# Expert stage: the first product of one tile issued in turn with the second product of the tile two behind it

## The reference, cut to what matters

```
logits = xn @ Wr + br;  top_p, top_idx = top_k(softmax(logits), 2);  weights = top_p / sum(top_p)
h = gelu(einsum('end,edh->enh', xn * ln_g + ln_b, W1) + b1)     # D=256 -> H=1024
y = einsum('enh,ehd->end', h, W2) + b2                          # H=1024 -> D=256
out = sum over the two chosen experts of weights * y;  x = x + out
```

## Time and profile before

| | us |
|---|---|
| median of 3 runs | 1185.47 (1185.44 to 1186.91) |
| the profiled execution | 1184.77 |
| its span in the trace | 1182.8 |
| expert stage, first `turn` to the last matmul | 821 to 1169 |
| TensorE busy over the span | 897.8 (76%) |
| VectorE, ScalarE, GpSimd busy | 740.9, 667.1, 671.8 |

### The profile page before, as it was taken

How to read it: one execution, slowest core, us unless ns; L and a number is a source line. 1 busy time by engine, 2 the same in 40 slices (tenths; PEclk the granted TensorE clock), 3 DMA queues, 4 the chain that set the end, 5 groups by cost and what they waited for, 6 DMA issues and landing times.

```text
span 1182.8 us, 25502 instructions
## 1 busy us (share of the span) xinstructions
PE 897.8 (76%) x6921; PEld 600.9 (51%) x6922; DVE 740.9 (63%) x1644; ACT 667.1 (56%) x2181; POOL 671.8 (57%) x678
## 2 busy tenths in 40 slices
PE   3284877687767866676776869525999999999995
PEld 1031433353324323354555648525777777777773
DVE  4667786878668755685556588865445555555543
ACT  7986996398935996352332336415444444444442
POOL 3753777767777777777773621326244444444442
PEclk9986997888878998686656889757999999999998
DMA  4113333443333333445442435411122222222221
GB/s 132 57 61 111 105 99 94 95 130 94 100 103 103 98 103 100 141 130 171 135 133 66 135 94 160 135 44 58 24 42 43 44 44 44 44 40 43 43 45 23
DMA packets 59608, 102.47 MB, mean 87 GB/s; under 512 B 10298, under 2 KB 43048, under 8 KB 59400
## 3 DMA queue, kind: packets, MB, share of 16 engines
q0 software_dynamic: 29520, 65.96, 23.0%
q1 hardware_dynamic: 30008, 35.55, 9.3%
HBM read 84.27 MB, written 17.20 MB: 86 GB/s over the span
## 4 chain that ended last, share of the span: by engine, by line
PE 46%; ACT 17%; DVE 16%; DMA 8%; issue 6%; POOL 4%; DVEq 2%; SPq 1%; POOLq 0%; ACTq 0%
ACT Wall L1045 10%; PE bank L979 9%; DMA Wall<-xl_d,gbuf 6%; PE bank L967 6%; PE bank L969 5%; PE bank L968 4%; ACT RB L1053 4%; PE bank L981 4%; POOL Wall L661 3%; PE bank L822 3%; PE bank L835 2%; PE bank L787 2%; PE bank L824 2%; PE bank L823 2%; DVE RA L1520 2%
## 5 line engine op out<-in xcount | busy, mean ns | idle before, releaser
L661 POOL DMA_INDIRECT Wall<-xl_d,gbuf x391 | 398.7, 1020 | 153.3 <-issue 75.9
L1053 ACT ACTIVATE RB<-RB,gbuf 128x128 f16<-128x128 f16 x488 | 178.4, 424 | 196.0 <-DVE RB L1507 196.0
L1045 ACT ACTIVATE Wall<-Wall 128x128 f32<-128x128 f16 (+1 forms) x782 | 246.5, 382 | 8.0 <-DVE Wall L1438 7.8
L822 PE MATMUL bank<-Wall,RB 128*128 x488 | 156.9, 322 | 113.6 <-DMA Wall<-xl_d,gbuf 44.6
L715 POOL DMA_INDIRECT out_dram<-RA,slot_tok x56 | 88.8, 1586 | 188.6 <-ACT RA L1171 181.6
L1520 DVE TENSOR_TENSOR RA<-RA,bank 128x256 f32 x244 | 101.9, 418 | 146.5 <-PE bank L824 135.4
L787 PE MATMUL bank<-Wall 128*128 128x512 f16 (+1 forms) x391 | 147.3, 421 | 30.3 <-ACT Wall L1045 24.3
L969 PE MATMUL bank<-RA,Wall 128*128 128x128 f16 x896 | 168.9, 223 | 0.0
L967 PE MATMUL bank<-RA,Wall 128*128 128x128 f16 x896 | 168.4, 223 | 0.5 <-issue 0.3
L968 PE MATMUL bank<-RA,Wall 128*128 128x128 f16 x896 | 166.6, 221 | 0.0
L822 PEld LDWEIGHTS bank<-Wall,RB 128*128 128x128 f16 x488 | 54.5, 112 | 213.4 <-issue 200.9
(11 more groups left out here) (314 smaller groups left out, 1570.6 us busy)
## 6 DMA issues: line engine op xcount, KB each, us to landing
stage<-in_L_ffn_W SPq DMA_DIRECT2D x10, 1024.0 KB, 5.2
Wall<-xl_d,gbuf POOLq DMA_INDIRECT x391, 2.8
Wall<-in_L_ffn_W SPq DMA_DIRECT2D x6, 1024.0 KB, 6.2
Wall<-in_x SPq DMA_DIRECT2D x4, 640.0 KB, 6.8
xl_d<-Wall SPq DMA_DIRECT2D x4, 640.0 KB
out_dram<-RB SPq DMA_DIRECT2D x4, 640.0 KB
xn_d<-RA SPq DMA_DIRECT2D x4, 640.0 KB
RB<-in_x SPq DMA_DIRECT2D x1, 1792.0 KB
```

Source lines behind the costliest of these rows:

```text
L661: pool.indirect_dma_start(out=ring[:, t % RING * 2 * D:(t % RING + 1) * 2 * D], out_offset=None, in_=xl_d, in_offset=bass.IndirectOffsetOn ...
L822: mm(o, high, ring[:, bass.ds(at, D)], start=True, stop=False)
L1045: last = act.activation(hi_word[:, n % SR, k * S:(k + 1) * S], hi_hot[:, n // HB % 2, n % HB // 2, 0:S, n % 2], ACT.Copy, scale=pay[k][:, ...
L1053: act.activation(low, high, ACT.Copy, scale=rec_r[:, n:n + 1]).then_inc(sw_built, 1)
```

## The change

The second product of tile t is issued in turn with the first product of tile t+2: an eighth of `up` (6 matmuls), an eighth of `down` (2 matmuls), eight times. For that `up` runs two tiles ahead instead of one, `turn` three instead of two, GpSimd's gather is moved one ahead (its fifth before the loop), and the orders of ScalarE and VectorE follow: `x_high(t+3)`, `gelu(t+2)`, `y_scale(t)`; `h_parts(t+1)`, `x_low(t+3)`, `y_rows(t)`. The word of a group holds 6 digits instead of 5. The number of matmuls and of tile buffers is the same. Before the loop now stand `up(0)` and `up(1)`; after it only `down` of the last two tiles stands alone.

```
@@ gpsimd
             for t in range(XR):
                 gather(t)
+            pool.wait_ge(ft_mm, 2 + 1)
+            gather(XR)
             for t in range(FT):
-                if t + XR < FT:
-                    pool.wait_ge(ft_mm, 2 + t + 1)
-                    gather(t + XR)
+                if t + XR + 1 < FT:
+                    pool.wait_ge(ft_mm, 2 + t + 2)
+                    gather(t + XR + 1)
@@ tensor
+            def up_part(t, q, e, hc):
+                if hc == 0:
+                    pe.wait_ge(fx_split, 2 + t + 1)
+                if hc % 4 == 0:
+                    pe.wait_ge(gelu_done, 2 * t + hc // 4 + 1)
+                o = bank[2 * q + hc // 4][:, (hc % 4) * P:(hc % 4) * P + P]
+                for kc in range(KC):
+                    w = [Wall[:, bass.ds(e + (part * KC + kc) * H + hc * P, P)] for part in range(2)]
+                    xh, xo = xhi[q][:, kc * P:kc * P + P], xlo[q][:, kc * P:kc * P + P]
+                    mm(o, w[0], xh, start=kc == 0, stop=False)
+                    mm(o, w[0], xo, start=False, stop=False)
+                    m = mm(o, w[1], xh, start=False, stop=kc == KC - 1)
+                if hc % 4 == 3:
+                    m.then_inc(up_mm, 1)
+
+            def down_part(t, q, ew2, hc):
+                if hc == 0:
+                    pe.wait_ge(y_out, t + 1)
+                    pe.wait_ge(h_split, 2 + t + 1)
+                w = Wall[:, bass.ds(ew2 + hc * 2 * D, 2 * D)]
+                hh, hl = hhi[q][:, hc * P:hc * P + P], hlo[q][:, hc * P:hc * P + P]
+                if hc == HC - 1:
+                    mm(bank[4 + q][:, 0:D], hl, Wall[:, bass.ds(ew2 + hc * 2 * D, D)], start=False, stop=False)
+                m = mm(bank[4 + q][:, 0:2 * D], hh, w, start=hc == 0, stop=hc == HC - 1)
+                if hc < HC - 1:
+                    mm(bank[4 + q][:, 0:D], hl, Wall[:, bass.ds(ew2 + hc * 2 * D, D)], start=False, stop=False)
+                else:
+                    m.then_inc(down_mm, 1)
...
+            def up_and_down(tu, qu, exu, td, qd, exd):
+
+                e = pe.snap(exu * WE)
+                ew2 = pe.snap(exd * WE + W2BASE)
+                for hc in range(HC):
+                    up_part(tu, qu, e, hc)
+                    down_part(td, qd, ew2, hc)
...
-            up(0, 0, experts(0)[0])
+            ex = experts(0)
+            up(0, 0, ex[0])
+            turn(2, 2, 1)
+            up(1, 1, ex[1])
             pe.wait_ge(w_done, 4 * NE)
             with pe.Fori(0, FT // XR - 1) as i:
                 ex = experts(i)
                 for q in range(XR):
-                    turn(XR * i + q + 2, (q + 2) % XR, i + 1 + (q + 2) // XR)
-                    up(XR * i + q + 1, (q + 1) % 2, ex[q + 1])
-                    down(XR * i + q, q % 2, ex[q])
+                    turn(XR * i + q + 3, (q + 3) % XR, i + 1 + (q + 3) // XR)
+                    up_and_down(XR * i + q + 2, q % 2, ex[q + 2], XR * i + q, q % 2, ex[q])
...
@@ scalar
                 for q in range(XR):
-                    x_high(XR * i + q + 2, q % 2)
-                    gelu(XR * i + q + 1, (q + 1) % 2, word, q + 1)
+                    x_high(XR * i + q + 3, (q + 1) % 2)
+                    gelu(XR * i + q + 2, q % 2, word, q + 2)
                     y_scale(XR * i + q, q % 2)
@@ vector
-            digit = [... for k in range(XR + 1)]
+            digit = [... for k in range(XR + 2)]
...
                 for q in range(XR):
-                    x_low(XR * i + q + 2, q % 2)
                     h_parts(XR * i + q + 1, (q + 1) % 2)
+                    x_low(XR * i + q + 3, (q + 1) % 2)
                     y_rows(XR * i + q, q % 2, word, q)
```

More of the change, by code:

```diff
@@ L952, in experts @@
             def experts(group):
-                word = pe.value_load(exp_tab[0:1, bass.ds(group, 1)], min_val=0, max_val=NE ** (XR + 1) - 1)
-                return [(word // NE ** k) % NE for k in range(XR + 1)]
+                word = pe.value_load(exp_tab[0:1, bass.ds(group, 1)], min_val=0, max_val=NE ** (XR + 2) - 1)
+                return [(word // NE ** k) % NE for k in range(XR + 2)]
+            def up_part(t, q, e, hc):
[12 more added lines that the diff above has]
+                    m.then_inc(up_mm, 1)
@@ L957, in up @@
             def up(t, q, ex):
                 e = pe.snap(ex * WE)
[L959 to L970, removed]
+                for hc in range(HC):
+                    up_part(t, q, e, hc)
@@ L972, in down @@
             def down(t, q, ex):
                 ew2 = pe.snap(ex * WE + W2BASE)
-                pe.wait_ge(y_out, t + 1)
-                pe.wait_ge(h_split, 2 + t + 1)
                 for hc in range(HC):
[L977 to L984, removed]
@@ L985, in down @@
-                m.then_inc(down_mm, 1)
+                    down_part(t, q, ew2, hc)
+            def up_and_down(tu, qu, exu, td, qd, exd):
+                e = pe.snap(exu * WE)
+                ew2 = pe.snap(exd * WE + W2BASE)
+                for hc in range(HC):
+                    up_part(tu, qu, e, hc)
+                    down_part(td, qd, ew2, hc)
+            assert HC == 8
             turn(0, 0, 1)
             turn(1, 1, 1)
-            up(0, 0, experts(0)[0])
+            ex = experts(0)
@@ L999, in _ @@
                 t = FT - XR + q
+                if t + 3 < FT:
+                    turn(t + 3, (t + 3) % XR, (t + 3) // XR + 1)
                 if t + 2 < FT:
[L1001 to L1004, removed]
+                    up_and_down(t + 2, t % 2, ex[q + 2], t, t % 2, ex[q])
+                else:
+                    down(t, t % 2, ex[q])
         @block.scalar
@@ L1156, in expert_word @@
             def expert_word(group):
-                return act.value_load(exp_tab[0:1, bass.ds(group, 1)], min_val=0, max_val=NE ** (XR + 1) - 1)
+                return act.value_load(exp_tab[0:1, bass.ds(group, 1)], min_val=0, max_val=NE ** (XR + 2) - 1)
             def gelu(t, q, word, k):
@@ L1174, in _ @@
             x_high(1, 1)
-            gelu(0, 0, expert_word(0), 0)
+            word = expert_word(0)
+            gelu(0, 0, word, 0)
+            x_high(2, 0)
+            gelu(1, 1, word, 1)
             with act.Fori(0, FT // XR - 1) as i:
@@ L1178, in _ @@
                 for q in range(XR):
-                    x_high(XR * i + q + 2, q % 2)
-                    gelu(XR * i + q + 1, (q + 1) % 2, word, q + 1)
+                    x_high(XR * i + q + 3, (q + 1) % 2)
+                    gelu(XR * i + q + 2, q % 2, word, q + 2)
                     y_scale(XR * i + q, q % 2)
             word = expert_word(FT // XR - 1)
[L1183 to L1188, removed]
+            for q in range(XR):
+                t = FT - XR + q
+                if t + 3 < FT:
+                    x_high(t + 3, (t + 3) % 2)
+                if t + 2 < FT:
+                    gelu(t + 2, t % 2, word, q + 2)
+                y_scale(t, t % 2)
         @block.vector
@@ L1713, in _ @@
             link(dve.memset(exp_row[:, FT:FT + XR], 0.0))
-            digit = [exp_row[:, k:k + FT].rearrange("p (g k) -> p g k", k=XR)[:, :, 0] for k in range(XR + 1)]
+            digit = [exp_row[:, k:k + FT].rearrange("p (g k) -> p g k", k=XR)[:, :, 0] for k in range(XR + 2)]
             words = exp_row[:, FT + XR:]
-            for k in range(XR, 0, -1):
-                link(dve.scalar_tensor_tensor(out=exp_tab[:, :] if k == 1 else words, in0=digit[XR] if k == XR else words,
+            for k in range(XR + 1, 0, -1):
+                link(dve.scalar_tensor_tensor(out=exp_tab[:, :] if k == 1 else words, in0=digit[XR + 1] if k == XR + 1 else words,
                                               scalar=float(NE), in1=digit[k - 1], op0=ALU.mult, op1=ALU.add))
@@ L1759, in expert_word @@
             def expert_word(group):
-                return dve.value_load(exp_tab[0:1, bass.ds(group, 1)], min_val=0, max_val=NE ** (XR + 1) - 1)
+                return dve.value_load(exp_tab[0:1, bass.ds(group, 1)], min_val=0, max_val=NE ** (XR + 2) - 1)
             def y_rows(t, q, word, k):
@@ L1774, in _ @@
             h_parts(0, 0)
+            x_low(2, 0)
             dve.wait_ge(b2_in, 16)
@@ L1784, in _ @@
                 t = FT - XR + q
-                if t + 2 < FT:
-                    x_low(t + 2, t % 2)
                 if t + 1 < FT:
                     h_parts(t + 1, (t + 1) % 2)
+                if t + 3 < FT:
+                    x_low(t + 3, (t + 3) % 2)
                 y_rows(t, t % 2, word, q)
```

## The result

| | before | after |
|---|---|---|
| median of 20 runs, us | 1184.22 | 1188.91 |
| ratio | | 1.004, 95% interval 1.0022 to 1.0059 |
| span of the profiled execution | 1182.8 | 1188.6 |
| a pass of the loop, mean of 12 | 24.26 | 24.41 |

The change made the kernel 4.7 us slower, by 2.6 to 7.0; 4.4 were forecast.

What follows compares the result with a forecast made beforehand. The prediction took TensorE's sequencer, not its array, to bound the expert stage; 2.5 + 0.1 + 0 + 1.8 = +4.4 us gave 1189.2 on the profiled execution, 1189.9 for the median, range 1183 to 1195.

Steps and rivals of the forecast that it cites:

- The bound: Expert stage: TensorE's sequencer sets the pass at 24.3 us, whatever the instructions' order; the array needs 21.96.
- (c): Waits between TensorE, ScalarE and VectorE in the loop: existing cover, 2.5 us ahead of `down`, suffices; 0 us.
- The first rival: Array itself pauses after each third first-product matmul, so long matmuls hide loads: some -31 us, 1154 us; chance 0.12.
- (a): `down` of a pass's first tile: two wait values computed afresh for one bare wait gone, 0.09 us a pass.
- (b): `down` of a pass's second tile: expert decoded again, six register operations instead of three, +0.10 us a pass.
- (d): Kernel's end: tile 53's scaling and output DMA come later, delaying the chain that ends last, +1.8 us.
- The pauses: TensorE's loop: pauses become smaller and more frequent, the period stays; tiles not first in a pass take 5.7 to 5.8 us.
- The last rival: TensorE alternating short and long matmuls: each change of kind costs array time, 1250 us, or 1199 at 0.03 us; chance 0.07.

Runs made afterwards that it cites:

- kernel 1: Changed kernel, both weight addresses of each three first-product matmuls computed in one register instruction, against the changed kernel: 22.29 us a pass, 1159.71 us, 0.9793 of before.
- kernel 8: Changed kernel plus one more address instruction in each eighth of the first product, same matmuls: 28.64 us a pass, 1.0456 of before.
- kernel 7: Changed kernel with fixed weight addresses on TensorE, the choice of expert left out in both products: 21.99 us a pass, 0.9787 of before.
- kernel 2: Kernel before, with both weight addresses of each three first-product matmuls computed in one register instruction: 23.81 us a pass, 1173.97 us, 0.9912 of before.
- kernel 4: Changed kernel, but at its end tile 53's second product and scaling go ahead of tile 55's first product and gelu: 1187.12 us, 1.0037 of before.
- kernels 3: Changed kernel with its new tile order, but eighths not in turn, all of up(t+2) then all of down(t): 1188.16 us, 1.0035 of before.
- kernel 5: Changed kernel with shared address instructions and new tile order, but eighths not in turn: 21.99 us a pass, 0.9787 of before.
- kernel 11: Changed kernel, eighths in turn, with shared address instructions and the old order at the end: 22.30 us a pass, 0.9799 of before.

## Why the prediction was right

- **The bound.** That the sequencer and not the array sets the changed kernel's pass was shown: 61 instructions fewer gave 2.1 us a pass (kernel 1), 32 more cost 4.23 (kernel 8), and none leaves the array's 21.99 (kernel 7). In the kernel before the same 61 are worth only 0.45 us a pass (kernel 2), for the reason under (c). The first rival, that the pause is the array's own, is out, and with it the pace of about 81 ns a matmul of the Trainium skill, page "TensorE: Matmul & The Clock Gate", section "Back-to-back issue gap", for this stream: 42 loads and matmuls ran at 0.0555 us before, and kernel 7's whole pass fits that pace.
- **(a) and (b).** Forecast +0.19 us a pass; measured 24.41 - 24.26 = 0.15, 13 passes +2.0 us for 2.5. The sequencer's rows show the added instructions at the places named.
- **(c).** The forecast of 0 held, but for a weaker reason than I gave, so partly by luck. I read a cover of 2.5 us ahead of `down` and took it for slack. But the chain through ScalarE and VectorE turns in 5.75 us, and the three tiles of a pass that have no branch took (24.26 - 7.00) / 3 = 5.75: there the two bounds are level. Only in the first tile did ScalarE wait for TensorE (both waits 12 times, once a pass, where it waited for VectorE 46 times, once a tile):

```profile
ACT RA L1171 <- DVE RA L1770: 134.2, 46, 3.0
ACT RA L1154 <- PE bank L969: 8.5, 12, 0.8
ACT RA L1165 <- PE bank L969: 2.5, 12, 0.3
```

  These are its waits between 860 and 1140 us: in total, times, longest. I read the cover as what that tile gives back in each pass; no run varied it. Over a pass the bounds are 24.26 and 23.81, one behind the other. The change took the second apart, which could not show while the first stood.
- **(d).** Forecast +1.8, measured +2.1 from the last matmul to the last DMA. The mechanism, a late scaling and then DMAs from landing to issue, is in the rows and starts where I put it: tile 53's DMA 3.1 us ahead of the last matmul's start, forecast (1166.3 and 1169.44) and measured (1170.00 and 1173.08). Each step from issue to issue was then put at 4.58 us; they measured 4.75 and 4.57. What I didn't see is how close ahead of it tile 52's DMA stands, so that kernel 4's repair of tile 53 alone gained nothing.
- **The pauses.** I wrote that they become smaller and more frequent, and that the tiles other than the first of a pass take 5.7 to 5.8 us. Both are wrong: they became fewer and larger, with one of 1.0 us at the branch, and the tiles take 5.69 to 6.66. In the kernel before, too, the pause after each third matmul runs through the first tile of a pass only. The sum over the pass, on which the forecast rests, isn't touched by it.
- **The last rival**, a price for each change of kind, is out by kernels 3 and 7.

2.0 + 2.1 = 4.1 of the 4.7 us of the medians, whose interval is 2.6 to 7.0. In the two profiled executions the stage from its first transposes (821.13 and 823.53) to the end of the span grew by 3.4 us: 1.8 between first and last branch, 2.1 behind the last matmul, -0.5 in the rest. The other 2.4 arose ahead of it and ahead of every line that the change touches: the same VectorE row there stands at 762.45 before (L1537) and at 764.96 after (L1564). So that 4.4 and 4.7 lie so close is in part luck; each of the terms is borne out to 0.5 us.

## What to carry to other kernels

Before reordering an engine's work, add up its sequencer's instructions: where they fill the period, order moves the pauses about and fewer instructions are what helps. When a bound is removed, look for the next one in the round of waits between engines, which can be each half busy; and judge a reordering with the first bound out of the way, since here the same change is worth +0.4% with it and -1.2% without. In this loop nothing was lost at the branch with a whole second product just ahead of it, and 0.3 us a pass with a mix of short and long matmuls; no run changed the lead alone.

## What the runs showed of the hardware

- A register instruction with three operations holds TensorE's sequencer for some 0.13 us (4.2 us for 32 before, 4.23 us a pass for 32 more in kernel 8), though its own row says 46 ns. One with six takes 74 ns by its row and replaces two.
- The sequencer's lead at a branch was 1.3 us with short and long matmuls mixed ahead of it (kernel 1) and 2.2 us with long ones alone (kernel 5).
- The chips ran the expert stage at the same pace (22.29 us a pass in kernel 1 on the first, 22.30 in kernel 11 on the third, the same loop) and the kernel before in medians of 1184, 1315 and 1313 us. The first branch of the loop came at 854 to 862 us on the first and at 979 to 999 on the other two.
